# The second residual of the FFN on VectorE, behind its rescaling, in a post-norm attention and int8 FFN kernel

## The reference

```python
x = layernorm(x + attention(x, Wq, Wk, Wv, Wo))
absmax = max(abs(x), axis=-1)
scale = maximum(absmax, 1e-7) / 127
q = clip(round(x / scale), -128, 127)
out = (q @ weight.T) * scale * w_scale + bias      # rounded to float16
x = layernorm(x + out.astype(float16))
```

## Time and profile before

| | us |
|---|---|
| median of 3 timed runs | 1356.7 (1356.2 to 1359.26) |
| the profiled execution | 1350.54 |
| its span, first to last instruction | 1348.8 |
| TensorE busy | 1277.5 (95%) |
| VectorE busy | 1041.9 (77%) |
| ScalarE busy | 898.6 (67%) |
| GpSimd busy | 392.6 (29%) |

### The profile page before, as it was taken

One profiled execution on the slowest core, in us unless ns is written; L12 is line 12 of the kernel. 1 busy time (PEld: TensorE's weight loads), 2 busy tenths in 40 slices (PEclk: granted clock), 3 DMA queues, 4 the chain that ended last, 5 costly groups with the idle time before them and its releaser, 6 DMA issues.

```text
span 1348.8 us, 17012 instructions
## 1 busy us (share of the span) xinstructions
PE 1277.5 (95%) x5840; PEld 940.1 (70%) x5840; DVE 1041.9 (77%) x1300; ACT 898.6 (67%) x1017; POOL 392.6 (29%) x454
## 2 busy tenths in 40 slices
PE   7899999999989999999998999999999899999795
PEld 5677776767757777677775777767776677777473
DVE  4598998874778888986579888888567888888565
ACT  4378778663667777865466867787346687779354
POOL 4232221112751121111383211121157211111266
PEclk9899999999999999999999999999999999999897
DMA  8784647394715364658632644548662445353641
GB/s 312 172 254 117 150 107 197 89 256 144 176 60 134 83 163 98 176 116 259 158 103 63 168 94 120 114 152 214 194 171 83 91 128 111 87 120 111 169 111 55
DMA packets 112403, 191.46 MB, mean 142 GB/s; under 512 B 19382, under 2 KB 65980, under 8 KB 104764
## 3 DMA queue, kind: packets, MB, share of 16 engines
q1 hardware_dynamic: 107708, 181.97, 51.4%
q10 hardware_dynamic: 4608, 8.39, 1.7%
HBM read 84.67 MB, written 38.54 MB: 91 GB/s over the span
## 4 chain that ended last, share of the span: by engine, by line
PE 84%; DVE 6%; issue 3%; ACT 2%; POOL 2%; DMA 1%; SPq 1%; ACTq 0%; POOLq 0%; DVEq 0%
PE ps L804 26%; PE ps L724 18%; PE ps L778 17%; PE ps L848 12%; PE ps L745 6%; PE ps L868 1%; DVE prob_hi L1221 1%; PE ps L824 1%; DVE xT L1162 1%; DMA y_scratch<-sums 1%; ACT probs L998 1%; POOL rstd L1445 1%; DVE stats L1301 1%; POOL f L1454 0%; PE ps L858 0%
## 5 line engine op out<-in xcount | busy, mean ns | idle before, releaser
L804 PE MATMUL ps<-prob_hi,v 128*65 128x512 f32 (+3 forms) x1280 | 412.6, 372 | 4.5 <-DVE prob_lo L1225 4.2
L998 ACT ACTIVATE probs<-ps 128x1024 f32<-128x1024 f32 x288 | 293.6, 1019 | 149.2 <-PE ps L778 146.2
L1225 DVE TENSOR_TENSOR prob_lo<-probs,prob_hi 128x1024 fp32r<-128x1024 f32 x288 | 363.9, 1264 | 9.9
L1430 POOL TENSOR_SCALAR_AFFINE_SELECT probs<-probs 128x256 f32<-128x256 f32 (+1 forms) x192 | 154.9, 814 | 724.1 <-ACT probs L1003 724.1
L778 PE MATMUL ps<-qk 128*128 128x512 f32 (+1 forms) x1280 | 315.3, 373 | 14.7 <-ACT probs L998 13.0
L1003 ACT ACTIVATE probs<-probs 128x1024 f32<-128x1024 f32 x288 | 305.7, 1061 | 9.8 <-ACT probs L1047 1.2
L724 PE MATMUL ps<-xT,w_ring 128*128 128x512 f32 x1152 | 289.9, 395 | 11.0 <-DVE xT L1162 6.1
L1221 DVE CAST prob_hi<-probs 128x1024 fp32r<-128x1024 f32 x288 | 212.6, 738 | 90.9 <-POOL probs L1430 53.4
L778 PEld LDWEIGHTS ps<-qk 128*128 128x128 f32 x1280 | 225.5, 189 | 74.3 <-ACT probs L998 15.6
L724 PEld LDWEIGHTS ps<-xT,w_ring 128*128 128x128 f32 x1152 | 217.1, 190 | 58.9 <-DVE xT L1162 7.4
L804 PE MATMUL ps<-prob_lo,v 128*65 128x512 f32 (+1 forms) x640 | 237.8, 372 | 0.0
(11 more groups left out here) (86 smaller groups left out, 967.1 us busy)
## 6 DMA issues: line engine op xcount, KB each, us to landing
qk<-work_r SPq DMA_DIRECT2D x64, 512.0 KB, 8.8
qk<-work_r SPq DMA_DIRECT2D x256, 128.0 KB, 2.7
y_scratch<-sums SPq DMA_DIRECT2D x128, 130.0 KB
wo<-wo_scratch SPq DMA_DIRECT2D x8, 2048.0 KB, 7.9
y_raw<-y_scratch SPq DMA_DIRECT2D x64, 256.0 KB, 4.2
w_ring<-w_scratch SPq DMA_DIRECT2D x12, 1024.0 KB, 6.8
x_raw<-X_T SPq DMA_DIRECT2D x16, 512.0 KB, 6.2
x_in<-X SPq DMA_DIRECT2D x32, 256.0 KB, 4.1
```

Of the source, the lines that this page charges most:

```text
L804: mm = nc.tensor.matmul(sums_ps[:, :, GQ - w:GQ], v[:, kt, v0:v0 + width], p[:, at, col:col + REP * w].rearrange("p (h q) -> p h q", h=REP ...
L998: nc.scalar.activation(probs[:, prob_place(g), :], scores[:, g % 2, :], ACT.Tanh, scale=SCORE_SCALE / SOFTCAP).then_inc(capped, 1)
L1225: nc.vector.tensor_tensor(prob_lo[:, prob_place(g), :], probs[:, prob_place(g), :], prob_hi[:, hi_place(g), :].bitcast(F32), ALU.subtract) ...
L1430: nc.gpsimd.affine_select(out=diag, in_=diag, compare_op=ALU.is_ge, fill=0.0, base=0, pattern=[[0, n], [1, P]], channel_multiplier=-1).the ...
```

## The change

The two adds of `residual2` move from GpSimd's list to VectorE's. On VectorE they stand right behind `rescale` of the same tile. Their waits, operands and the semaphores that they raise are the same.

```diff
@@ block.vector
+            def residual2(b, t):
+                dve.wait_ge(scaled, rows_upto(b, t))
+                if t == 0:
+                    dve.wait_ge(bias_loaded, bias_upto(b))
+                if t >= 1:
+                    dve.wait_ge(x2_done, rows_upto(b, t - 1))
+                nc.vector.tensor_tensor(f16[:, :], ffn_tile(t), bias[:, :], ALU.add).then_inc(biased, 1)
+                dve.wait_ge(biased, rows_upto(b, t))
+                nc.vector.tensor_tensor(ffn_tile(t), f16[:, :], row_tile(t), ALU.add).then_inc(x2_done, 1)
...
                     if t >= 3:
                         rescale(b, t - 3)
+                        residual2(b, t - 3)
                     shift_by(b, t - 1, 0, rstd1, shift1)
...
                 rescale(b, NT - 3)
+                residual2(b, NT - 3)
                 shift_by(b, NT - 1, 0, rstd1, shift1)
...
                 rescale(b, NT - 2)
+                residual2(b, NT - 2)
                 shift_by(b, NT - 3, 1, rstd2, shift2)
...
                 rescale(b, NT - 1)
+                residual2(b, NT - 1)
                 shift_by(b, NT - 2, 1, rstd2, shift2)
@@ block.gpsimd
-            def residual2(b, t):
...
-                nc.gpsimd.tensor_tensor(f16[:, :], ffn_tile(t), bias[:, :], ALU.add).then_inc(biased, 1)
-                pool.wait_ge(biased, rows_upto(b, t))
-                nc.gpsimd.tensor_tensor(ffn_tile(t), f16[:, :], row_tile(t), ALU.add).then_inc(x2_done, 1)
...
                     inverse_std(b, t - 1, 0, mv1, veps1, rstd1, z_done)
-                    if t >= 3:
-                        residual2(b, t - 3)
                     if t + 1 < NT:
                         split_y(b, t + 1)
```

More of the change, by code:

```diff
@@ L1509, in _ @@
                 inverse_std(b, NT - 1, 0, mv1, veps1, rstd1, z_done)
-                residual2(b, NT - 3)
                 inverse_std(b, NT - 3, 1, mv2, veps2, rstd2, normed)
@@ L1513, in _ @@
                     mask(b + 1, 0)
-                residual2(b, NT - 2)
                 inverse_std(b, NT - 2, 1, mv2, veps2, rstd2, normed)
@@ L1517, in _ @@
                     mask(b + 1, 1)
-                residual2(b, NT - 1)
                 inverse_std(b, NT - 1, 1, mv2, veps2, rstd2, normed)
```

## The result

| | before | after |
|---|---|---|
| median of the timed runs, us | 1356.45 (1355.36 to 1359.26) | 1364.93 (1364.32 to 1366.72) |
| profiled execution / its span | 1350.54 / 1348.8 | 1364.45 / 1361.7 |
| VectorE / GpSimd busy | 77% / 29% | 79% / 23% |

The change makes the kernel slower: ratio 1.0072, 95% interval 1.0048 to 1.0095 (the quotient of the two medians alone is 1.0063, inside that interval). 1369.6 was forecast, in a range of 1360 to 1378.

The account below looks back on a forecast made before the run. TensorE was taken as the bound (84% of the wait chain), except at the closing stage's end. 7.5 boundaries + 0.6 bias + 3.5 tail + 1.3 clock = 12.9 us, on the 1356.7 median: 1369.6 us, range 1360 to 1378.

Parts of the forecast that it names:

- The price of an add: Each moved add of 128x512 on VectorE takes 0.69 us, with bounds of 0.35 and 1.29.
- The lap: Closing stage: wait chain VectorE-ScalarE-GpSimd-VectorE grows from 6.75 to 7.93 us, over TensorE's 7.40 turn; last turn's shift 3.3 late.
- The wait for the bias: Batch 1: the bias lands late and VectorE, instead of GpSimd, waits for it with its whole queue, +0.6 us.
- The boundary: End of a batch into the next: +2.4 to 2.5 us each, three of them, 7.5 together.
- the wait for the mask: Batch end: VectorE's 0.7 us wait for GpSimd's mask of the next batch's probabilities was to go.
- the product at tile 7 would be missed by about 1.0: Batch end: VectorE, wanting to rescale tile 7, comes 1.0 us before its FFN product is ready.
- The clock: TensorE idles before tile 7's FFN product, which then runs at 1.2 GHz level: 0 to 2.5 us over three boundaries, 1.3 taken.
- The tail: After the last batch, no probabilities to win on: 4.6 us late up to the last FFN product, less 1.1: +3.5.
- the first rival: GpSimd's later steps are early enough, the lap doesn't close, slip stays 1.2 instead of 3.3: about 1360 us; chance 0.12.
- the add isn't 0.35: Second rival: VectorE does each add in 0.35 us, the lap stays hidden: -9 us, 1347.8; chance 0.03.
- the casts don't stay slow: Fourth rival: the boundary's disturbed casts have another cause and stay slow: 11 us more, 1380; chance 0.07.
- The 10.9 us of waits for GpSimd's adds: Third rival: VectorE's 24 waits for these adds all lie on the path; their going would give 1345.8; chance 0.06.

Follow-up runs that it names:

- the memsets: The changed kernel with two unneeded GpSimd memsets of 128x400 added behind the mask of the next batch's first group; one profiled execution, no time compared.

## Why the prediction was right

- **The price of an add.** 0.69 us taken, 0.69 measured (692 ns over the 32 first adds; of the second adds only those beside the mask took 0.78). From rescaling to shift 2.10 against 2.11.
- **The lap.** 7.93 us forecast, 7.93 measured, with each of its parts within 0.03 us, and the quarter-width adds bring it back under the turn. TensorE does stall for q every turn. At turn 7 the forecast was 3.3 late, or 3.9 in batch 1 with the bias's 0.6; 3.17 to 3.59 came, 3.50 in batch 1. The wait for the second 1/std was put at about 0.5 us and is 0.74.
- **The wait for the bias.** Taken as 0.6 in batch 1. The trace of the changed kernel has two waits for it, 0.7 us together and 0.4 the longest. That it would be waited for in batch 0 as well was missed (the first shift of turn 3 slips 1.52 us there, 1.08 in batch 2), and the mark of batch 1 shows only 0.33 more than those of batches 2 and 3.
- **The boundary.** The FFN product of tile 7 was forecast 4.6 us later in batch 0; by the count of the marks it starts 4.63 later (391.49 less 335.92, against 387.85 less 336.91). Forecast +4.6 at the second shift of tile 5, 4.1 after tile 7's pair, 2.4 to 2.5 at the end. Batch 2 gave 4.22, 3.90 and 2.12. The casts fell back as forecast. Wrong in detail: the wait for the mask didn't go (0.41 us of 0.75 stayed), because the two mask passes took 1.85 us together instead of 1.00. VectorE's adds beside them are the cause: with tiles 0 to 5 moved, where no add of VectorE runs there, the passes take 1.00 us in all three batches, and with tiles 6 and 7 moved 1.84. That the product at tile 7 would be missed by about 1.0 held roughly: the rescaling waits 0.65 us for it in batch 1, at full clock, and 1.50 in batch 0, at the slow one.
- **The clock.** 1.3 us over three boundaries; the product took 1.89, 1.04 and 1.15 us, together 0.96 more than 3 x 1.04. When the change was run again it was 1.55, 1.89 and 1.04, which is 1.36 more.
- **The tail.** +3.5 forecast, +3.25 measured.
- **The sum.** The terms for the closing stages came to 12.9 us, the marks give 11.0: each term is somewhat too large, the lap's end least, the boundaries most (7.5 + 0.6 + 1.3 = 9.4 against 7.8). The spans also differ by 12.9, but that agreement is chance and not these steps: 2.5 us of it lie in the attention part of batch 2, where the granted clock was 0.74 of full speed from 897 to 903 us against 1.00 in before's profile at 893 to 900, and 1.0 us was won at the start. That part, whose instructions are the same in all kernels here, took 266.4 us in before's profile and from 266.6 to 269.8 in the others; what lowers the clock there isn't settled. The timed medians (+8.5 and +11.4) fit the 11.0 better. The forecast of 1369.6 is thus 4.7 us above the measured median, and 1364.93 lies about as near to the first rival's 1360; what tells them apart is the lap in the trace, not the time.
- **The rivals.** The lap closes, the add isn't 0.35, the casts don't stay slow. The 10.9 us of waits for GpSimd's adds did go, and the kernel still lost: most of them stood ahead of idle time of VectorE. The rule of the Trainium skill that elementwise work with two inputs belongs on VectorE (GPSIMD Engine Reference, Engine selection) holds for the single instruction (0.69 against 1.29 us). For the kernel it depends on the place: all adds behind scale_y, or only those of tiles 6 and 7 in either place, made it slightly faster, the other three placements of full-width adds slower.

## What to carry to other kernels

Before moving work into an engine's idle time, write down the lap that runs through that place: every step that waits for the next, over all engines, back to the same instruction of the next tile. If the lap with the new work exceeds the bound engine's turn, the excess comes back every turn, however idle the engine looked. The same work behind the instruction that the others wait for can cost nothing: here, in the loop, two places in one queue with only a shift and a scaling between them (1.3 us) differ by 3.0 to 3.5 us at turn 7 of an undisturbed batch, and the whole kernels (whose last tiles were moved too) by some 14 us.

## What the runs showed of the hardware

VectorE and GpSimd hold each other up when certain of their instructions overlap. A VectorE add with two SBUF inputs went from 0.69 to 1.32 and to 2.74 us beside GpSimd's 2.4 us split; in the second case it ended 0.56 us after the split did, as if it had waited for its end. GpSimd suffers as well: one-element steps went from 0.18 to 0.65 and from 0.55 to 1.01, a memset from 0.43 to 0.86, two mask passes from 1.00 to 1.85. The Trainium skill (SBUF — State Buffer, Who interferes with whom) says so of two-input VectorE operations beside GpSimd operations that read SBUF, and of VectorE in a two-port mode beside GpSimd. The rows agree: the memsets, which read nothing, left the two-input split alone, and traded delays with the cast. I had thought of small steps of GpSimd delaying an add; what I hadn't expected is that the adds would delay steps of one element per partition, and that this decides places: ahead of the statistics the adds cost 31 us, behind the rescaling 11, behind scale_y less than nothing.
